# A CIN tower on one core: three fp32r passes for four of six first-layer chunks, an earlier warm-up and VectorE chain, and rows put in place by SyncE's transfers

## The chip, the cores and the metric

The kernel runs on one core of a Trainium2 chip, as one launch. The core has TensorE (matmuls into PSUM), VectorE, ScalarE, GpSimd, SyncE (here only as an issuer of transfers) and 16 DMA engines; SBUF and PSUM have 128 partitions each. The metric is the device time of the launch in microseconds, the median of several runs. A profiled execution has its own time, given beside its span.

## The reference, cut to what is computed

```python
e = jnp.stack([tbl_f[ids[:, f]] for f in range(39)], axis=1)      # (1024, 39, 16)
x1 = relu(einsum('bhd,bmd,shm->bsd', e, e, W1) + b1)              # S = 128
x2 = relu(einsum('bhd,bmd,shm->bsd', x1, e, W2) + b2)             # S = 128
z  = concatenate([x1.sum(-1), x2.sum(-1)], axis=-1)               # (1024, 256)
h = concatenate([z, dense_ctx], axis=1)                           # + 16 columns
h = maximum(h @ W_top1 + b_top1, 0)                               # 512
h = maximum(h @ W_top2 + b_top2, 0)                               # 256
y = h @ W_top3                                                    # (1024, 1)
```

All of it is fp32.

## The kernel before

**Tiles.** The batch is cut into 32 tiles of 32 examples. A tile has 32 x 16 = 512 columns of (example, embedding position) for the first layer. For the second layer it is two "pairs" (p = 2t even, 2t + 1 odd) of two blocks ("sub") of 128 columns each. A pair is the unit of every engine's main loop.

**Rows.** GpSimd looks up the embedding rows with indirect DMAs into `looked` (ten for a tile, 64 bytes a row; L339). A row then has to be put in place, into `e`, where positions are spread over partitions: 16 copies of 32 partitions x 40 elements for a tile (`put_in_place`, L290). For tiles 0 and 1 VectorE does eight of them (L561) and ScalarE eight (L464); for later tiles ScalarE does all 16. Tiles are put, split into high and low parts and multiplied in "fills": one tile a fill up to tile 7, two tiles up to 19, four tiles from 20 (`FILLS`). A fill is worked at the even pair two tiles ahead of its first tile: ScalarE puts at slots 1, 3, 4 and makes the high part after slot 5; VectorE computes products after its D bank 4 (L570) and the low parts after D bank 5 (L580, L583).

**First layer.** The 741 products of two fields left after 15 that are made directly are written as squares of sums: TensorE expands x0t with a selection matrix into one of six chunks (`expand`, L690, fp32r, 512 columns), ScalarE squares it from PSUM to SBUF (`square`, L444), and TensorE multiplies it with the weights in fp32 (`layer1`, L702) into the bank BK_ACC1. Expand(t, v+1) and layer1(t, v) follow each other on TensorE, two slots after expand(t, v). All expansions, the turn of the next tile (`turn`, L678), the sums and the dense layers share one PSUM bank, BK_T: `staging` makes each use wait until the one before it has been read. After the last chunk ScalarE makes x1h and x1 (L450, L453), VectorE x1l (L595, after D bank 3 of the even pair).

**Second layer.** For each of 39 fields TensorE multiplies x1 with W2 in three fp32r passes (x1h w2h, x1h w2l, x1l w2h; L724 to L726), four fields to a bank. Of the ten banks of a pair seven (27 fields, "D") are scaled and added up by VectorE (L634, one multiply-add of 128 columns for each field and sub, `acc`), and three (12 fields, "A") are scaled by ScalarE into `fy` (L425) and added by GpSimd (L348) into `fsum`, with which VectorE's chain starts. The order on TensorE is the string `ORDER = "DDADDADDAD"`, ten slots a pair; the A banks are made one pair and one bank ahead. Banks go through a ring of three: bank n waits until bank n - 3 has been read. First-layer steps stand in every second slot: expansions of chunks 0 to 4 in slots 1, 3, 5, 7, 9 of the odd pair, chunk 5 in slot 1 of the next even pair, and the last layer1 in slot 3.

**Start.** TensorE folds the weights (L761), turns tile 0, runs its first layer, and then makes the banks A0, A1, A2 of pair 0 and the first A bank of pair 1 before the loop. VectorE splits W2 into w2h and w2l in between (L588, L590).

**Dense layers.** They run for examples 0 to 511 in tiles 17 and 18, for 512 to 895 in tiles 29 and 30, the rest at the end (`MLP_AT`).

## Time and profile before

| | us |
|---|---|
| median of 3 runs (1232.1 to 1232.55) | 1232.25 |
| the profiled execution | 1228.31 |
| its span | 1226.4 |
| TensorE busy | 1172.4 (96%) |
| VectorE busy | 1005.4 (82%) |
| ScalarE busy | 672.1 (55%) |
| GpSimd busy | 864.8 (71%) |

The busy shares are averages over the span. The chain of work that ended last says which engine's work stood where the end was set. The order of time lists instructions of an engine with start and length, merged where they follow each other without a pause; an idle time before one is given in brackets with what ended it. A length holds the pipeline's tail, so the distance of two starts is the cost of one where they are packed. A matmul's column count stands behind its partitions.

### The profile page before, as it was taken

What the parts mean: (1) busy time and instruction counts of PE and PEld (TensorE: products, weight loads), DVE (VectorE), ACT (ScalarE), POOL (GpSimd) and SP (SyncE); (2) the same over time, 40 slices, a digit from 0 to 9 for tenths busy, and PEclk for the clock granted to TensorE, in tenths of its full rate; (3) what the DMA queues carried; (4) which work ended last, traced back from release to release, by engine and by line L of the source; (5) the groups of instructions that cost most, each with busy time, mean ns of one, the idle gap of its engine ahead of it and who ended that gap; (6) DMA issues with size and microseconds to landing.
All of it is one profiled execution on the core that took longest, in us unless ns stands there. A gap on an engine that the chain in (4) does not pass through costs nothing.

```text
span 1226.4 us, 17749 instructions
## 1 busy us (share of the span) xinstructions
PE 1172.4 (96%) x4784; PEld 879.4 (72%) x4784; DVE 1005.4 (82%) x3692; ACT 672.1 (55%) x2188; POOL 864.8 (71%) x836
## 2 busy tenths in 40 slices
PE   3899999999999999999999999999999999999996
PEld 2577777777777777777776667777777777777775
DVE  4298898888899888888896678888888888887695
ACT  2656666665565656556564465555655565545430
POOL 7888878888888788788776757888886454444350
PEclk9899999999999999999999999999999999999997
DMA  5000000000000000000000000000000000000000
GB/s 177 5 4 4 4 4 3 4 4 5 3 4 3 4 3 3 4 4 3 4 4 3 3 3 3 4 3 4 3 4 2 1 1 1 1 1 1 1 1 1
DMA packets 12801, 9.08 MB, mean 7 GB/s; under 512 B 6190, under 2 KB 11822, under 8 KB 12573
## 3 DMA queue, kind: packets, MB, share of 16 engines
q0 software_dynamic: 10240, 2.64, 2.6%
q1 hardware_dynamic: 2461, 5.31, 1.3%
q8 instruction: 38, 0.62, 0.2%
q14 instruction: 62, 0.51, 0.1%
HBM read 7.92 MB, written 0.00 MB: 6 GB/s over the span
## 4 chain that ended last, share of the span: by engine, by line
PE 72%; DVE 18%; ACT 5%; issue 2%; POOL 2%; DMA 0%; SPq 0%; ACTq 0%
PE ps L724 17%; PE ps L726 17%; PE ps L725 17%; DVE acc L634 15%; PE ps L702 13%; PE ps L690 3%; PE ps L755 3%; ACT e L464 2%; ACT fy L425 2%; POOL looked L339 2%; DVE x1l L595 1%; PE ps L678 1%; DVE e_hl L580 1%; PE ps L697 0%; DVE e_hl L583 0%
## 5 line engine op out<-in xcount | busy, mean ns | idle before, releaser
L634 DVE SCALAR_TENSOR_TENSOR acc<-ps,e,acc 128x128 f32<-128x128 f32 x3200 | 854.4, 343 | 155.7 <-PE ps L726 152.4
L724 PE MATMUL ps<-w2h,x1h 128*128 128x512 f32 (+1 forms) x1280 | 582.4, 455 | 24.9 <-ACT fy L425 13.8
L348 POOL TENSOR_TENSOR fy<-fy 128x512 f32<-128x512 f32 (+1 forms) x256 | 403.0, 1574 | 214.3 <-ACT fy L425 193.5
L425 ACT ACTIVATE fy<-ps,e 128x128 f32<-128x128 f32 x1536 | 418.1, 387 | 198.8 <-PE ps L726 198.3
L726 PE MATMUL ps<-w2h,x1l 128*128 128x512 f32 (+1 forms) x1280 | 495.4, 387 | 0.0
L725 PE MATMUL ps<-w2l,x1h 128*128 128x512 f32 (+1 forms) x1280 | 494.3, 386 | 0.0
L339 POOL DMA_INDIRECT looked<-in_table,rows x320 | 310.9, 972 | 79.1 <-issue 55.0
L724 PEld LDWEIGHTS ps<-w2h,x1h 128*128 128x128 f32 x1280 | 241.5, 189 | 134.1 <-DVE acc L634 50.9
L725 PEld LDWEIGHTS ps<-w2l,x1h 128*128 128x128 f32 x1280 | 241.6, 189 | 82.6 <-issue 44.7
L726 PEld LDWEIGHTS ps<-w2h,x1l 128*128 128x128 f32 x1280 | 240.7, 188 | 48.4
L444 ACT ACTIVATE z<-ps 128x512 f32<-128x512 f32 x192 | 117.9, 614 | 224.8 <-PE ps L690 219.5
L702 PE MATMUL ps<-z,w_sb 128*128 128x512 f32 x384 | 198.8, 599 | 0.0
L702 PEld LDWEIGHTS ps<-z,w_sb 128*128 128x128 f32 x384 | 73.4, 192 | 16.6 <-ACT z L444 1.7
L690 PE MATMUL ps<-x0t,sel_r 78*128 78x512 f32 x186 | 74.0, 398 | 2.7 <-ACT z L444 1.8
L464 ACT ACTIVATE e<-looked 32x40 f32<-32x40 f32 (+5 forms) x256 | 67.3, 263 | 13.7 <-DMA looked<-in_table,rows 7.8
L348 POOL TENSOR_TENSOR fy<-fy,b_sb 128x256 f32<-128x256 f32 x64 | 47.7, 746 | 18.8 <-ACT fy L425 17.8
L634 DVE SCALAR_TENSOR_TENSOR acc<-ps,e,fsum 128x128 f32<-128x128 f32 x128 | 38.8, 344 | 26.0 <-POOL fsum L348 16.8
L348 POOL TENSOR_TENSOR fsum<-fy 128x256 f32<-128x256 f32 x64 | 47.5, 743 | 10.8 <-POOL fy L348 4.4
L690 PEld LDWEIGHTS ps<-x0t,sel_r 78*128 78x128 f32 x186 | 34.9, 188 | 10.9 <-ACT z L444 3.5
L634 DVE SCALAR_TENSOR_TENSOR ps<-ps,e,acc 128x128 f32<-128x128 f32 x128 | 38.9, 350 | 0.0
L432 ACT ACTIVATE x0t<-ps 128x512 fp32r<-128x512 f32 x32 | 19.4, 605 | 30.5 <-PE ps L678 30.5
L678 PE MATMUL ps<-ident_sb,e_hl 128*128 128x128 f32 x128 | 20.9, 287 | 9.1 <-DVE e_hl L583 8.8
(64 smaller groups left out, 385.5 us busy)
## 6 DMA issues: line engine op xcount, KB each, us to landing
looked<-in_table,rows POOLq DMA_INDIRECT x320, 2.3
w_st<-in_w SPq DMA_DIRECT2D x1, 1728.0 KB, 10.2
wt_sb<-in_wt SPq DMA_DIRECT2D x2, 512.0 KB
w_st<-in_w SPq DMA_DIRECT2D x1, 768.0 KB, 6.3
w_sb<-in_w1a SPq DMA_DIRECT2D x1, 448.0 KB, 3.2
w1b_sb<-in_w1b SPq DMA_DIRECT2D x1, 448.0 KB, 3.8
...
```

What stands on the lines that cost most here:

```text
L339: nc.gpsimd.indirect_dma_start(looked[:, t % LOOKED, j, :], None, table, bass.IndirectOffsetOnAxis(rows[:, t, j:j + 1], 0)).then_inc(s_loo ...
L348: nc.gpsimd.tensor_tensor(out, a, b, ALU.add).then_inc(s_fsum, 1)
L425: nc.scalar.activation(fy[:, p % 2, sub, m - MD, :], ps[:, 2 * (nth % RING) + sub, k * S:(k + 1) * S], ACT.Copy, scale=emb(p, sub, m)).the ...
L444: nc.scalar.activation(z1[:, k % 2, :], src, ACT.Square).then_inc(s_z1, 1)
L464: nc.scalar.activation(*put_in_place(f, k, q), ACT.Copy).then_inc(s_put_act, 1)
L634: nc.vector.scalar_tensor_tensor(acc[:, sub, :] if m < MD - 1 else y, y, emb(p, sub, m), acc[:, sub, :] if m else fsum[:, p % 2, sub, :], ...
L690: nc.tensor.matmul(ps[:, BK_T, :], sel_r[:, v, :], x0t[0:2 * M, t % 2, :], start=True, stop=True).then_inc(s_full, 1)
L702: nc.tensor.matmul(ps[:, BK_ACC1, :], w1_sb[:, v, :], z1[:, k % 2, :], start=False, stop=(v == C1 - 1)).then_inc(s_mm1, 1)
L724: nc.tensor.matmul(y, x1h[:, t % 2, at], w2h[:, cols], start=True, stop=False)
L725: nc.tensor.matmul(y, x1h[:, t % 2, at], w2l[:, cols], start=False, stop=False)
L726: mm = nc.tensor.matmul(y, x1l[:, t % 2, at], w2h[:, cols], start=False, stop=True)
L755: mm = nc.tensor.matmul(y, w, x, start=(k == 0), stop=(k == len(terms) - 1))
```

## The change

- **Three passes.** For tiles from 2 on, chunks 0, 2, 3, 5 of the first layer (`SPLIT`) are no longer multiplied in fp32. The weights are split once into w1h and w1l (fp32r), the squares into zh (ScalarE, fp32r) and zl: ScalarE squares a second time in place in PSUM (`s_sq`), and VectorE subtracts zh from it into zl (`square_low`). TensorE then does w1h zh + w1l zh + w1h zl. `staging` waits for VectorE's subtraction (`s_zl`) in these chunks. `split_after` puts the subtraction into VectorE's program after a D bank: D bank 1, 3 and 5 of the odd pair for chunks 0, 2, 3, and D bank 1 of the even pair for chunk 5.
- **Warm-up and first banks.** 28 matmuls of 512 columns with no use stand before turn(0). The order of banks of pair 0 is new: A0, D0, A1, D1, A2 before the loop, then nine more. For the first two pairs (`LATE`) VectorE's chain starts with a multiplication and adds fsum later, before its last field. The first bank waits for x1l only at its third matmul. The split of W2's A part is shared: ScalarE makes w2h, VectorE w2l.
- **Rows.** For tiles from 2 on SyncE puts the rows in place with 16 DMAs a tile from `looked` to `e`, after the tile's look-ups; ScalarE, VectorE and GpSimd wait for `s_put`.
- **Moved.** Dense-layer steps stand in other slots; hid1, hid2 and y_sb lie in the memory of w2_st.

```diff
+SPLIT, SPLIT_FROM = (0, 2, 3, 5), 2
+LATE = 2
+WARM = 28
...
-    slots = [[("A", 0, a) for a in range(A_BANKS)] + [("A", 1, a) for a in range(EARLY)]]
-    for p in range(PAIRS):
+    slots = [[("A", 0, 0), ("D", 0, 0), ("A", 0, 1), ("D", 0, 1), ("A", 0, 2)]]
...
+    for p in range(1, PAIRS):
...
+def split_after(p, j):
+
+    slots = [s for s, kind in enumerate(ORDER) if kind == "D"] + [SLOTS]
+    return [at for s in range(slots[j], slots[j + 1]) for at in layer1_steps(p, s) if is_split(*at)]
...
-    for c, s in enumerate((0, 4, 14, 16)):
+    for c, s in enumerate((0, 4, 8, 14)):
...
-    MLP_AT[TILE_SLOTS * (tile + 1) + 14] = (g, 3, 0)
+    MLP_AT[TILE_SLOTS * (tile + 1) + 8] = (g, 3, 0)
...
+                for t in range(FIRST_TILES, TILES):
+                    sp.wait_ge(s_look[t], 16 * LOOKUPS)
+                    for k in range(Q):
+                        for q in range(Q):
+                            sp.dma_start(*put_in_place(t, k, q)).then_inc(s_put[t - FIRST_TILES], 16)
...
-                    nc.scalar.activation(z1[:, k % 2, :], src, ACT.Square).then_inc(s_z1, 1)
+                    if is_split(t, v):
+                        nc.scalar.activation(zh[:, k % 2, :], src, ACT.Square).then_inc(s_z1, 1)
+                        nc.scalar.activation(src, src, ACT.Square).then_inc(s_sq, 1)
+                    else:
+                        nc.scalar.activation(z1[:, k % 2, :], src, ACT.Square).then_inc(s_z1, 1)
...
+                def square_low(t, v):
+                    k = C1 * t + v
+                    dve.wait_ge(s_sq, splits(t, v))
+                    if k >= 2:
+                        dve.wait_ge(s_mm1, k - 1)
+                    nc.vector.tensor_tensor(zl[:, k % 2, :], ps[:, BK_T, :], zh[:, k % 2, :], ALU.subtract).then_inc(s_zl, 1)
...
+                            if m == MD - 1 and p < LATE:
+                                dve.wait_ge(s_fsum, ADDS_PER_PAIR * (p + 1))
+                                dve.wait_ge(s_stt, n)
...
+                        for at in split_after(p, j):
+                            square_low(*at)
...
-                            pe.wait_ge(s_z1, C1 * at[0] + at[1] + 1)
+                            if is_split(*at):
+                                pe.wait_ge(s_zl, splits(*at))
+                            else:
+                                pe.wait_ge(s_z1, C1 * at[0] + at[1] + 1)
...
+                    if is_split(t, v):
+                        nc.tensor.matmul(ps[:, BK_ACC1, :], w1h[:, v, :], zh[:, k % 2, :], start=False, stop=False)
+                        nc.tensor.matmul(ps[:, BK_ACC1, :], w1l[:, v, :], zh[:, k % 2, :], start=False, stop=False)
+                        pe.wait_ge(s_zl, splits(t, v))
+                        mm = nc.tensor.matmul(ps[:, BK_ACC1, :], w1h[:, v, :], zl[:, k % 2, :], start=False, stop=(v == C1 - 1))
...
+                for _ in range(WARM):
+                    nc.tensor.matmul(ps[:, C1 - 1, :], sel_r[:, 0, :], sel_r[:, 0:N // K1, :].rearrange("p c k -> p (c k)"),
+                                     start=True, stop=True)
```

TensorE, odd pair 1, from the last matmuls of bank D2 over the expansion of chunk 1 of tile 2 and the multiplication of chunk 0 to bank D3 (ps is PSUM, z the squares, sel_r the selection matrix; the semaphores an instruction waits for stand in brackets). Before:

```order
L724 MATMUL ps<-w2h,x1h 128x512
L725 MATMUL ps<-w2l,x1h 128x512
L726 MATMUL ps<-w2h,x1l 128x512
L690 MATMUL ps<-x0t,sel_r 128x512 [waits s_z1]
L702 MATMUL ps<-z,w_sb 128x512 [waits s_z1]
L724 MATMUL ps<-w2h,x1h 128x512 [waits s_stt]
```

Now:

```order
L796 MATMUL ps<-w2h,x1h 128x512
L797 MATMUL ps<-w2l,x1h 128x512
L800 MATMUL ps<-w2h,x1l 128x512
L752 MATMUL ps<-x0t,sel_r 128x512 [waits s_zl]
L765 MATMUL ps<-zh,w1h 128x512 [waits s_z1]
L766 MATMUL ps<-zh,w1l 128x512
L768 MATMUL ps<-zl,w1h 128x512 [waits s_zl]
L796 MATMUL ps<-w2h,x1h 128x512 [waits s_stt]
```

The expansion waits for s_zl, VectorE's subtraction, where it waited for s_z1, ScalarE's square, and three matmuls stand for one.

VectorE, the same pair, banks D0, D1 and D2. Before:

```order
L634 SCALAR_TENSOR_TENSOR acc<-ps,e,fsum 128x128 [waits s_stt,s_fsum,s_y]
L634 SCALAR_TENSOR_TENSOR acc<-ps,e,fsum 128x128 [waits s_stt,s_fsum]
L634 SCALAR_TENSOR_TENSOR acc<-ps,e,acc 128x128 [waits s_stt] x6
L634 SCALAR_TENSOR_TENSOR acc<-ps,e,acc 128x128 [waits s_stt,s_y]
L634 SCALAR_TENSOR_TENSOR acc<-ps,e,acc 128x128 [waits s_stt] x7
L634 SCALAR_TENSOR_TENSOR acc<-ps,e,acc 128x128 [waits s_stt,s_y]
```

Now (L688 multiplies, L691 multiplies and adds, L633 is the subtraction):

```order
L688 TENSOR_SCALAR acc<-ps,e 128x128 [waits s_stt,s_y]
L688 TENSOR_SCALAR acc<-ps,e 128x128 [waits s_stt]
L691 SCALAR_TENSOR_TENSOR acc<-ps,e,acc 128x128 [waits s_stt] x6
L691 SCALAR_TENSOR_TENSOR acc<-ps,e,acc 128x128 [waits s_stt,s_y]
L691 SCALAR_TENSOR_TENSOR acc<-ps,e,acc 128x128 [waits s_stt] x7
L633 TENSOR_TENSOR zl<-ps,zh 128x512 [waits s_mm1,s_sq]
L691 SCALAR_TENSOR_TENSOR acc<-ps,e,acc 128x128 [waits s_stt,s_y]
L691 SCALAR_TENSOR_TENSOR acc<-ps,e,acc 128x128 [waits s_stt] x7
```

The subtraction stands between bank D1 and bank D2 and waits for ScalarE's second square.

VectorE, the first banks of pair 0. Before:

```order
L583 TENSOR_TENSOR e_hl<-prod,e_hl 128x60 [waits s_eh]
L634 SCALAR_TENSOR_TENSOR acc<-ps,e,fsum 128x128 [waits s_fsum,s_y]
L634 SCALAR_TENSOR_TENSOR acc<-ps,e,fsum 128x128 [waits s_fsum]
L634 SCALAR_TENSOR_TENSOR acc<-ps,e,acc 128x128 [waits s_stt] x6
L634 SCALAR_TENSOR_TENSOR acc<-ps,e,acc 128x128 [waits s_stt,s_y]
```

Now:

```order
L620 TENSOR_TENSOR e_hl<-prod,e_hl 128x60 [waits s_eh]
L688 TENSOR_SCALAR acc<-ps,e 128x128 [waits s_y]
L688 TENSOR_SCALAR acc<-ps,e 128x128
L691 SCALAR_TENSOR_TENSOR acc<-ps,e,acc 128x128 [waits s_stt] x6
L691 SCALAR_TENSOR_TENSOR acc<-ps,e,acc 128x128 [waits s_stt,s_y]
L691 SCALAR_TENSOR_TENSOR acc<-ps,e,acc 128x128 [waits s_stt] x7
```

The wait for s_fsum is gone from the chain's head; only the bank itself (s_y) is waited for.

## Rows read from the trace of the kernel before

**Rows 1.** The page's busy line, and the chain's shares by engine.
```profile
PE 1172.4 (96%) x4784; PEld 879.4 (72%) x4784; DVE 1005.4 (82%) x3692; ACT 672.1 (55%) x2188; POOL 864.8 (71%) x836
...
PE 72%; DVE 18%; ACT 5%; issue 2%; POOL 2%; DMA 0%; SPq 0%; ACTq 0%
```

**Rows 2.** The chain in time: start us, us, what; VectorE's multiply-adds, every second pair.
```profile
380.22 1.96 DVE acc L634 x8
...
415.09 1.96 DVE acc L634 x8
...
451.06 1.96 DVE acc L634 x8
```

**Rows 3.** Order of time, TensorE, an ordinary tile: start us, us, engine, line, operation.
```profile
458.08 0.50 PE L724 MATMUL ps<-w2h,x1h 128*128 128x512 f32 x1 [0.27 <-DVE acc L634]
...
461.44 0.40 PE L690 MATMUL ps<-x0t,sel_r 78*128 78x512 f32 x1
...
464.64 0.40 PE L690 MATMUL ps<-x0t,sel_r 78*128 78x512 f32 x1
...
464.87 1.02 PE L702 MATMUL ps<-z,w_sb 128*128 128x512 f32 x2
...
465.96 0.40 PE L725 MATMUL ps<-w2l,x1h 128*128 128x512 f32 x1
...
475.82 0.40 PE L690 MATMUL ps<-x0t,sel_r 78*128 78x512 f32 x1
```

**Rows 4.** Order of time, VectorE, the same tile.
```profile
453.14 0.68 DVE L595 SCALAR_TENSOR_TENSOR x1l<-ps,x1h 128x512 fp32r<-128x512 f32 x1
...
453.80 5.26 DVE L634 SCALAR_TENSOR_TENSOR acc<-ps,e,acc 128x128 f32<-128x128 f32 x20
...
460.01 0.60 DVE L634 SCALAR_TENSOR_TENSOR acc<-ps,e,fsum 128x128 f32<-128x128 f32 x2
...
471.13 4.23 DVE L634 SCALAR_TENSOR_TENSOR acc<-ps,e,acc 128x128 f32<-128x128 f32 x16 [1.66 <-PE ps L726]
```

**Rows 5.** Order of time, a fill of two tiles: VectorE, then TensorE's expand(t, 1).
```profile
422.17 1.17 DVE L580 TENSOR_TENSOR e_hl<-e,e_hl 128x312 f32<-128x312 f32 x1
...
423.25 0.82 DVE L583 TENSOR_TENSOR e_hl<-prod,e_hl 128x120 f32<-128x120 f32 x1
...
426.07 0.60 DVE L634 SCALAR_TENSOR_TENSOR acc<-ps,e,fsum 128x128 f32<-128x128 f32 x2
...
429.76 0.40 PE L690 MATMUL ps<-x0t,sel_r 78*128 78x512 f32 x1
```

**Rows 6.** Order of time, a fill of one tile: VectorE, then TensorE's expand(t, 1).
```profile
107.58 0.60 DVE L634 SCALAR_TENSOR_TENSOR acc<-ps,e,fsum 128x128 f32<-128x128 f32 x2
...
111.52 0.40 PE L690 MATMUL ps<-x0t,sel_r 78*128 78x512 f32 x1
```

**Rows 7.** Order of time, a fill of four: VectorE, then TensorE's expand(t, 1).
```profile
871.22 0.60 DVE L634 SCALAR_TENSOR_TENSOR acc<-ps,e,fsum 128x128 f32<-128x128 f32 x2
...
875.38 0.40 PE L690 MATMUL ps<-x0t,sel_r 78*128 78x512 f32 x1
```

**Rows 8.** The start: a stretch with its granted clock (0.50), then order of time.
```profile
37.00:38.30 1.30, 1.30 (x4) 0.99 (x3) 0.99 (x5) 1.18 (x6) 0.99 (x2) 0.50 0.10 8
...
38.99 6.30 ACT L425 ACTIVATE fy<-ps,e 128x128 f32<-128x128 f32 x24
...
56.06 0.61 DVE L634 SCALAR_TENSOR_TENSOR acc<-ps,e,fsum 128x128 f32<-128x128 f32 x2 [16.76 <-POOL fsum L348]
...
73.01 0.40 PE L690 MATMUL ps<-x0t,sel_r 78*128 78x512 f32 x1
```

**Rows 9.** Transfers: the look-ups' queue, two issues of SyncE, the last look-up of tile 2.
```profile
q0 software_dynamic: 10240, 2.64, 2.6%
...
18.81 0.90 SPq L327 DMA_DIRECT2D wt_sb<-in_wt  x2
...
46.54 0.94 POOL L339 DMA_INDIRECT looked<-in_table,rows  x1 [0.30 <-issue]
```

151 lines of the change are left out of this document (91 added, 60 removed).

## The prediction

> **What bounds the kernel now.** I read the page's busy shares first, then the chain of work that ended last, then the order of time on TensorE and VectorE over two tiles. [rows 1] TensorE is busy 96% of the span and holds 72% of the chain; VectorE is busy 82% and holds 18%. That reads like a TensorE-bound kernel, and for such a kernel cheaper matmuls are worth their full saving. But 18% of the chain is VectorE, so a part of each tile is set by it. [rows 2] gives the tile's period: the same point of every second pair comes at 380.22, 415.09 and 451.06, so 34.87 us for a tile without a fill ahead of it and 35.97 us for one with a fill of two tiles.
>
> I call T the start of expand(t, 0), which follows the second D bank of an odd pair. [rows 3] In an ordinary tile T is 461.44. TensorE then wants expand(t, 1) at 464.64, T + 3.20, and expand(t, 4) at 475.82. [rows 4] VectorE starts D bank 0 of that pair at 460.01, T - 1.43. One multiply-add costs 5.17/20 = 0.2585 us (20 of them from 453.80 to 458.97, the row's 5.26 less its overlapping end), so a D bank of eight is 2.07 us against 1.37 us for TensorE to make one. VectorE ends D bank 1 at 460.01 + 4.14 = 464.15. This lag, not the busy share, is what the change meets.
>
> **Three passes for one fp32 matmul.** [rows 3] One fp32r matmul of 512 columns is 0.23 us (464.64 to 464.87). From 464.87 to 465.96 stand the fp32 matmul and one fp32r matmul, so the fp32 one is 1.09 - 0.23 = 0.86. Three passes are 0.68: 0.18 saved, 4 x 30 tiles = 120 times, 21.6 us if nothing else moves.
>
> What it adds: 120 squares on ScalarE, written back to the PSUM bank (of the size of those already there, on a ScalarE that is 55% busy and loses its copies; only the subtraction waits for them), and 120 subtractions on VectorE of 128x512 from PSUM. That operation is not in the trace; x1l has its shape and its kinds of operands, and takes 453.80 - 453.14 = 0.66 us [rows 4]. I take 0.66. The bounds: x1l and a multiply-add of 128 columns differ by 384 columns and 0.40 us, so 512 columns without any fixed part are 0.53; four multiply-adds of 128 columns would be 1.03. In sum 79 us more for VectorE.
>
> **The added wait.** There is one staging bank (BK_T). Before, expand(v+1) waits until ScalarE has squared chunk v; that is done while the next bank is multiplied. Now it waits for VectorE's subtraction, which stands in VectorE's program behind a D bank. Queued behind that expand on TensorE are all further banks. A release from VectorE costs TensorE about 0.25 us: D bank 5 ended at 453.80 + 16 x 0.2585 = 457.94 and the bank that waited for it started at 458.08, with its first matmul some 0.11 longer [rows 3, 4]. The four places, in an ordinary tile:
> - chunk 0: VectorE ends D bank 1 at 464.15, subtraction 464.81, release 465.06, wanted 464.64. Lost 0.42.
> - chunk 2: VectorE starts D bank 4 at 471.13 after an idle gap of 1.66 us [rows 4]; the subtraction fits there. Lost 0.
> - chunk 3: it stands behind D bank 5. From 471.13 (now 0.24 later) two banks and a subtraction end at 476.17, release 476.42. TensorE, with 0.42 - 0.18 - 0.18 behind it, wants it at 475.88. Lost about 0.55.
> - chunk 5: it stands behind D bank 1 of the even pair; three banks later TensorE only just finds it ready. Lost 0, and the 0.18 saved counts, because VectorE waits for the bank behind it. (The wait for D bank 5 at the next pair's first bank, the idle 0.27 in [rows 3], stays.)
> Sum: 0.97 lost against 0.72 saved, so +0.25 us in an ordinary tile.
>
> **After a fill it is worse**, since VectorE enters the odd pair later and before the ring of three banks hid most of it. For each kind I take VectorE's start of D bank 0, add 4.14 + 0.66 + 0.25, and compare with the time at which TensorE took expand(t, 1) before:
> - fill of two [rows 5]: the low parts run from 422.17 to 424.00; 426.07 + 5.05 = 431.12 against 429.76: 1.36 lost. Over the ordinary 0.42 that is 0.94 more, so +1.19 a tile, 6 tiles: +7.1.
> - fill of one [rows 6]: 107.58 + 5.05 = 112.63 against 111.52: 1.11 lost, +0.94 a tile, 5 tiles: +4.7.
> - fill of four [rows 7]: 871.22 + 5.05 = 876.27 against 875.38: 0.89 lost, +0.72, 2 tiles: +1.4. The copies that ScalarE made there go, but behind them VectorE's chain is next in line, so they give nothing here.
> - ordinary: 12 tiles x 0.25 = +3.0.
> - the four tiles with dense-layer steps: TensorE has extra work, VectorE time to spare; the moved steps give slack at one place and take it at another. Taken as 0, between -2 and +2.
> Together +16.2 us.
>
> The low parts have a price of their own in this: [rows 5] 128x312 takes 1.08 us (422.17 to 423.25) where its size would ask for about a third. If that time vanished in the new kernel's timing, a fill would cost 0.7 less, 11 x 0.7 = 8 us.
> The Trainium skill's page "SBUF — State Buffer", section "SBUF: two separate sides", gives a reason: an operation of VectorE with two SBUF inputs and a GpSimd operation take one port pair in turn, each for its whole length. By that rule the length stays as it is, since GpSimd's additions keep their place; without it the sum would be 8 us lower. No run here shows which.
>
> **The start.** [rows 8] VectorE's first multiply-add stands at 56.06, after 16.76 us of idle time for GpSimd's fsum; T of the first odd pair is 73.01. Now D banks come between the A banks and need no fsum. What is late next: put(1) hangs on the look-ups, and ScalarE reads its first bank at 38.99 whatever TensorE did before. So the 28 warm-up matmuls and the earlier first bank are worth little: TensorE makes banks A0, D0, A1 by about 36, then waits until ScalarE's bank has been read, at 38.99 + 6.30/3 = 41.1, and the granted clock may be down by then (0.50 from 37.0 to 38.3 [rows 8]). The warm-up stands in a stretch in which TensorE waits for turn(0) anyway; if all 28 ran at half clock, 0.46 us each, and ended some us after turn(0) could start, the same wait for ScalarE would hide it. From 41.1 on TensorE has D1, turn(1), A2, the seven chunks of tile 1, nine more banks and D0, D1 of pair 1: 1.3 for the slow clock, 0.5 + 6.8 + 0.5 for turns and chunks, 13 banks at 1.37 less 0.3, and about 1.3 of waits for ScalarE's squares while it scales A2: 28 us, T at about 69. Gain 4 us; bounds 0 (the clock stays down through these gaps) and 8 (none of the waits).
>
> **Rows put in place by SyncE.** Per tile 16 DMAs of 320 runs of 16 bytes; ScalarE loses its copies of tiles 2 to 31, which stood on no end-setting path except in fills of four. [rows 9] Two issues of SyncE take 0.90, so 16 take 7.2 us, plus about 2.3 to land. Tile 2's look-ups end at about 49.8: in place at 59.3, wanted by VectorE (products after D bank 4) near 61. Later tiles have a pair, some 17 us, to spare. So 0 is the price taken. It is bounded from above by the runs: 10,240 packets of four rows took 2.6% of 16 engines, 510/10,240 = 0.05 us a packet, 0.0125 a row. At 0.0125 a run a tile's 5,120 runs take 4 us on 16 engines; at a whole packet's 0.05 they take 16 us, and tile 2 is 7 us late. SyncE's queue holds nothing else but the output.
> The Trainium skill speaks against this part: "DMA: Bandwidth & Descriptors", section "Specifications", says that below 512 bytes a transfer is a read-modify-write. By that rule 16-byte runs lie at the dear end, and the sum would be 7 us higher; its section "Why small descriptors are slow (HBM only)" says that transfers within SBUF are spared, which would leave 0. No transfer within SBUF is in this trace.
>
> **The sum.** 1228.31 (profiled execution, span 1226.4) - 4 + 16.2 = 1240.5. The median of the runs is 1232.25, 3.9 above the profiled one; 1232.25 + 12.2 = 1244.
>
> **The rivals.**
> A. TensorE alone sets the pace: the subtractions find gaps everywhere (VectorE idles 155 us in all), 21.6 + 4 are gained: 1207. For it: 96% busy. Against it: VectorE's gaps lie behind D bank 1 and ahead of D bank 4, while three of four subtractions are wanted elsewhere [rows 4].
> B. The waits are only half paid, because VectorE's low parts shorten or because releases come at 0.14 and not 0.25: 16.2 - 8 - 6, near +2, with the start -2: 1230, from 1225 to 1236.
> C. Slower still: the puts land late. It decides from a put of more than 9 us a tile; at 16 us tile 2 is 7 us late and VectorE stands at products(2), at 32 us, close to the 34.9 us period, it is 23 us late and the next fills follow. 1244 + 7 to 20, taken as 1255.
> My own forecast ends above the time before, A below.
>
> **Chances.** Forecast 0.60 (its own range, with start and low parts at their bounds, 1234 to 1254), A 0.16, B 0.12, C 0.12. A measurement of this kernel tells 0.2%, 2.5 us, from no change. Faster: all of A, half of B, a little of mine: 0.23. Same: 0.07. Slower: 0.70. The range that leaves out two in ten cuts most of A and the end of C: 1216 to 1258.
>
> **What would show it.** Right: VectorE busy near 1085 us; TensorE's busy time a little down yet its idle time up, the expansion (now line 752) waiting for VectorE's subtraction about twice a tile for 0.4 to 1.4 us; tile periods of about 35.1, and near 37.1 where a fill of two precedes; VectorE's first multiply near 41; the copies' landing ahead of line 607. Wrong: expansions that never wait and a period of 34.2 (A); high_part or products waiting for a DMA (C); first T later than 73. The step I trust least is the carry of a fill's lateness into the odd pair, the most secure the 0.66 us of the subtraction.

## The result, and the profile after

The changed kernel takes 1262.18 us (median of four, 1260.91 to 1264.23) against 1232.4 (four, 1232.1 to 1233.03): ratio 1.0243, 95% interval 1.0225 to 1.026. It is slower, as forecast, but by 30 us where 12 were forecast, and the time lies above the range of 1216 to 1258. The profiled execution is the one of 1260.91, its span is 1259.1.

The page of the changed kernel: busy time by engine, the SyncE queue's packets, the shares of the chain, and groups of instructions (busy, mean ns | idle before, and what ended it). The answers of before are in [rows 1].

```profile
PE 1175.3 (93%) x4932; PEld 905.1 (72%) x4932; DVE 1090.3 (87%) x3816; ACT 667.0 (53%) x2070; POOL 866.0 (69%) x836
...
q1 hardware_dynamic: 159901, 7.73, 7.1%
...
PE 52%; DVE 38%; issue 6%; ACT 2%; POOL 1%; another core or an unknown queue 0%; DMA 0%; SPq 0%; DVEq 0%; ACTq 0%
...
L796 PE MATMUL ps<-w2h,x1h 128*128 128x512 f32 (+1 forms) x1280 | 535.0, 418 | 39.5 <-DVE acc L691 29.4
...
L633 DVE TENSOR_TENSOR zl<-ps,zh 128x512 fp32r<-128x512 f32 x120 | 81.8, 682 | 21.3 <-ACT ps L480 20.8
L752 PE MATMUL ps<-x0t,sel_r 78*128 78x512 f32 x186 | 79.8, 429 | 19.6 <-DVE zl L633 10.0
```

The subtraction costs 682 ns (forecast 0.66 us), and VectorE is busy 1090 (forecast 1085). TensorE's busy time rose from 1172.4 to 1175.3; without the 6.8 of the warm-up matmuls it fell by 3.9. Its share of the chain went from 72% to 52%, VectorE's from 18% to 38%. Part of TensorE's new idle time stands where the forecast put it, at the expansion (L752). There it waits 35 times for the subtraction, 1.0 us at the most. More stands at L796, the first pass of a bank, and it is VectorE's banks that release it: 29.4 us. In before that was 7.9.

Where the time went is read from T, the start of the matmul that follows expand(t, 0), once a tile. Two pairs of rows of that line on TensorE (start, duration), of the changed kernel: behind a fill of one, and in an ordinary tile.

```profile
156.21 0.39 PE L759 MATMUL ps<-x0t,wz 128*128 128x512 f32 x1
...
193.81 0.39 PE L759 MATMUL ps<-x0t,wz 128*128 128x512 f32 x1
...
832.53 0.39 PE L759 MATMUL ps<-x0t,wz 128*128 128x512 f32 x1
...
867.56 0.39 PE L759 MATMUL ps<-x0t,wz 128*128 128x512 f32 x1
```

That is 37.60 us behind a fill of one, against 35.15, and 35.03 in an ordinary tile, against 34.84 (836.17 - 801.33). The forecast had 36.1 and 35.1. The first T of an odd pair is 82.45 against 73.25, where 69 was forecast (its counterpart of 73.01; the two lines stand 0.24 apart). Of the 32.6 us between the two profiled executions 9.2 lie ahead of the first T of an odd pair, 12.6 in the six periods behind it (five fills of one, the first of two) and 11.3 in the next ten (five fills of two); the others together add nothing. So the ordinary tile came out right, the fills and the start did not. Here is one fill of the changed kernel, all engines that matter (start, duration, engine, line):

```profile
148.15 0.95 POOL L371 DMA_INDIRECT looked<-in_table,rows  x1 [0.30 <-issue]
...
148.89 1.62 DVE L607 TENSOR_TENSOR prod<-e 128x60 f32<-128x60 f32 x1
...
149.10 2.72 POOL L380 TENSOR_TENSOR fy<-fy 128x512 f32<-128x512 f32 x2
...
150.43 2.15 DVE L691 SCALAR_TENSOR_TENSOR acc<-ps,e,acc 128x128 f32<-128x128 f32 x8
...
152.50 0.40 DVE L617 TENSOR_TENSOR e_hl<-e,e_hl 128x156 f32<-128x156 f32 x1
...
152.63 0.50 PE L796 MATMUL ps<-w2h,x1h 128*128 128x512 f32 x1 [1.80 <-DVE acc L691]
```

The product of 60 elements takes 1.62 us; in before it takes 0.21. It stands ahead of D bank 5, and that bank holds the PSUM that TensorE's next bank needs: TensorE idles 1.80 us.

### The profile page after: what moved, and what is told of

Read it like the earlier page. It is cut to its first block, busy times and chain, and to the rows that moved or that the text cites. A ratio compares the mean times of both kernels' runs of the same rounds, so it can differ in the third digit from the quotient of the medians.

```text
span 1259.1 us, 18613 instructions
## 1 busy us (share of the span) xinstructions
PE 1175.3 (93%) x4932; PEld 905.1 (72%) x4932; DVE 1090.3 (87%) x3816; ACT 667.0 (53%) x2070; POOL 866.0 (69%) x836
## 4 chain that ended last, share of the span: by engine, by line
PE 52%; DVE 38%; issue 6%; ACT 2%; POOL 1%; another core or an unknown queue 0%; DMA 0%; SPq 0%; DVEq 0%; ACTq 0%
DVE acc L691 31%; PE ps L796 12%; PE ps L800 11%; PE ps L797 11%; PE ps L770 4%; PE ps L752 4%; PE ps L829 3%; DVE zl L633 3%; PE ps L765 2%; PE ps L768 2%; PE ps L766 2%; DVE prod L607 2%; DVE x1l L637 1%; ACT fy L459 1%; POOL looked L371 1%
## 5 line engine op out<-in xcount | busy, mean ns | idle before, releaser
L691 DVE SCALAR_TENSOR_TENSOR acc<-ps,e,acc 128x128 f32<-128x128 f32 x3200 | 852.5, 342 | 82.7 <-PE ps L800 71.7
L796 PE MATMUL ps<-w2h,x1h 128*128 128x512 f32 (+1 forms) x1280 | 535.0, 418 | 39.5 <-DVE acc L691 29.4
L796 PEld LDWEIGHTS ps<-w2h,x1h 128*128 128x128 f32 x1280 | 242.0, 189 | 123.8 <-DVE acc L691 57.8
L479 ACT ACTIVATE zh<-ps 128x512 fp32r<-128x512 f32 x120 | 71.7, 598 | 211.8 <-PE ps L752 187.1
L633 DVE TENSOR_TENSOR zl<-ps,zh 128x512 fp32r<-128x512 f32 x120 | 81.8, 682 | 21.3 <-ACT ps L480 20.8
L752 PE MATMUL ps<-x0t,sel_r 78*128 78x512 f32 x186 | 79.8, 429 | 19.6 <-DVE zl L633 10.0
L770 PE MATMUL ps<-z,w_sb 128*128 128x512 f32 x144 | 75.9, 609 | 0.0
L480 ACT ACTIVATE ps<-ps 128x512 f32<-128x512 f32 x120 | 71.1, 593 | 0.0
L752 PEld LDWEIGHTS ps<-x0t,sel_r 78*128 78x128 f32 x186 | 34.8, 187 | 47.3 <-DVE zl L633 28.3
L482 ACT ACTIVATE z<-ps 128x512 f32<-128x512 f32 x72 | 45.5, 632 | 20.5 <-PE ps L752 12.9
L691 DVE SCALAR_TENSOR_TENSOR acc<-ps,e,fsum 128x128 f32<-128x128 f32 x124 | 37.6, 344 | 17.3 <-PE ps L800 7.7
L765 PE MATMUL ps<-zh,w1h 128*128 128x512 f32 x120 | 47.8, 398 | 0.0
```

The costliest lines, as they stand in the source:

```text
L479: nc.scalar.activation(zh[:, k % 2, :], src, ACT.Square).then_inc(s_z1, 1)
L633: nc.vector.tensor_tensor(zl[:, k % 2, :], ps[:, BK_T, :], zh[:, k % 2, :], ALU.subtract).then_inc(s_zl, 1)
L691: nc.vector.scalar_tensor_tensor(acc[:, sub, :] if m < MD - 1 else y, y, emb(p, sub, m), acc[:, sub, :] if m else fsum[:, p % 2, sub, :], ...
L752: nc.tensor.matmul(ps[:, BK_T, :], sel_r[:, v, :], x0t[0:2 * M, t % 2, :], start=True, stop=True).then_inc(s_full, 1)
L765: nc.tensor.matmul(ps[:, BK_ACC1, :], w1h[:, v, :], zh[:, k % 2, :], start=False, stop=False)
L770: mm = nc.tensor.matmul(ps[:, BK_ACC1, :], w1_sb[:, v, :], z1[:, k % 2, :], start=False, stop=(v == C1 - 1))
```

## What each kernel showed

All kernels of this study by the same places. The ratio is to the kernel before, run on the same chip between them. Its median was 1232.4 beside the changed kernel, 1232.1 beside undo_passes, only_passes, only_puts and only_start, 1232.7 beside copies_twice and the three mid_ kernels, and 1227.0 or 1227.2 beside all others. First T is that of the first odd pair; "one" is the period from the fifth T to the sixth, behind a fill of one; "two" the two tiles with one fill of two (tenth T to twelfth); "ordinary" from the 23rd to the 24th; "four" the next, behind a fill of four. All in us of the profiled execution.

| kernel | ratio (95%) | first T | one | two | ordinary | four |
|---|---|---|---|---|---|---|
| before | 1 | 73.25 | 35.15 | 70.85 | 34.84 | 36.25 |
| after | 1.0243 (1.0225-1.026) | 82.45 | 37.60 | 72.70 | 35.03 | 36.73 |
| undo_passes | 1.0105 (1.0075-1.0134) | 84.99 | 36.35 | 71.42 | 34.86 | 36.40 |
| only_passes | 1.0181 (1.0149-1.0212) | 79.20 | 36.19 | 72.27 | 35.00 | 38.48 |
| only_puts | 1.0055 (1.0035-1.0075) | 76.67 | 36.32 | 71.42 | 34.87 | 37.97 |
| only_start | 1.0058 (1.0035-1.0081) | 88.15 | 35.14 | 70.80 | 34.86 | 36.21 |
| only_mlp | 0.9988 (0.9976-0.9999) | 72.42 | 35.15 | 70.83 | 34.87 | 36.21 |
| puts_prod_early | 1.0148 (1.0095-1.02) | 72.89 | 38.23 | 71.82 | 34.87 | 36.95 |
| passes_mid | 0.9912 (0.9883-0.9941) | 73.12 | 34.82 | 70.12 | 34.25 | 36.16 |
| no_warm | 1.0226 (1.0197-1.0256) | 75.45 | 37.71 | 72.80 | 35.01 | 36.73 |
| after_mid | 1.0066 (1.0043-1.0089) | 75.39 | 37.32 | 71.62 | 34.25 | 37.50 |
| puts_two_waits | 1.0054 (1.0031-1.0077) | 73.49 | 36.32 | 71.40 | 34.87 | 36.41 |
| only_warm | 1.0006 (0.9995-1.0017) | 71.77 | 35.12 | 70.82 | 34.86 | 36.20 |
| only_order | 1.0026 (1.0012-1.004) | 79.22 | 35.12 | 70.82 | 34.86 | 36.20 |
| copies_twice | 0.9979 (0.9967-0.9991) | 78.27 | 35.14 | 70.83 | 34.89 | 36.25 |
| mid_0 | 1.0015 (1.0004-1.0026) | 77.18 | 35.22 | 71.03 | 34.67 | 36.59 |
| mid_03 | 0.9895 (0.9867-0.9924) | 77.58 | 34.86 | 70.12 | 34.25 | 36.19 |
| mid_2late | 0.9953 (0.9934-0.9973) | 76.98 | 35.06 | 70.53 | 34.46 | 36.42 |
| puts_add_waits | 0.9972 (0.996-0.9984) | 72.26 | 35.15 | 70.80 | 34.86 | 36.06 |
| all_mended | 0.9859 (0.9842-0.9875) | 72.58 | 34.83 | 69.90 | 34.22 | 35.43 |

A caution for "first T": where the kernel before ran at 1232, kernels with its start have it some 5 us later (copies_twice 78.27) than where it ran at 1227 (only_mlp 72.42). The profiled execution of before, 3.9 under its median, is of the latter kind. First T is compared only within a kind: the changed kernel's 82.45 belongs beside the 78.27 of copies_twice, not beside 73.25.

A caution for "four" too. After much the same wait TensorE's granted clock fell in some of these periods and not in others, whatever the kernel. In only_passes TensorE waits 2.21 us for ScalarE in both fills of four. After the first wait the clock was 0.50, the lower level of 1.2 GHz, for some 3 us; after the second it stayed at 1.00 (a stretch; busy time and instructions of TensorE, its weight loads, VectorE, ScalarE and GpSimd; granted clock; DMA share and GB/s):

```profile
888.47 0.55 PE L801 MATMUL ps<-w2h,x1h 128*128 128x512 f32 x1 [2.21 <-ACT fy L462]
...
1032.69 0.47 PE L801 MATMUL ps<-w2h,x1h 128*128 128x512 f32 x1 [2.21 <-ACT fy L462]
```

```profile
889.00:892.00 3.00, 3.00 (x10) 2.52 (x9) 2.77 (x3) 1.36 (x6) 2.69 (x3) 0.50 0.00 0
1033.00:1036.00 3.00, 3.00 (x16) 2.65 (x15) 3.00 (x5) 2.42 (x11) 2.69 (x3) 1.00 0.00 0
```

Ten matmuls stand where 16 do at the full clock. This is in the 38.48 of only_passes (its second fill of four took 36.93, where before took 36.22) and in the 37.97 of only_puts (clock 0.52 from 881 to 884.5; puts_two_waits took 36.41); both are some 1.5 too long as a price of the kernel. The 37.50 of after_mid holds such a stretch too (0.50 from 883 to 886). No other value of the column does.

## One part at a time

Theory M: the start and VectorE's subtractions are the loss. Rivals: SyncE's transfers, or the extra preparation.

**undo_passes:** the changed kernel, no chunk split, w1h and w1l not made.

```diff
-SPLIT, SPLIT_FROM = (0, 2, 3, 5), 2
+SPLIT, SPLIT_FROM = (), 2
```

> All parts of the change but the three passes (no chunk is split, and w1h and w1l are not made). Theory M (the loss of about 30 us is 9 at the start and the rest from VectorE's subtractions behind the banks and the fills): the start's 9 us stays, the period of every tile goes back to that of before, 34.9 ordinary and 35.15 after a fill of one: 1241, within 3. Rival S (SyncE's transfers of 16-byte runs disturb the other engines' access to SBUF, and the fills' lateness comes from them): periods after fills of one stay near 37, 1250 or more. Rival D (the start's delay comes from the extra preparation of w1h and w1l, 7 us of instructions on ScalarE and VectorE): near 1233.

**only_passes:** the changed kernel with the bank order, the prologues and the copies by ScalarE and VectorE as before; left of the change are the passes and the dense-layer steps.

```diff
-LATE = 2
+LATE = 0
-PUT_DVE, PUT_ACT = (0, 1), (2, 3)
+def put_by_act(f):
+    return tuple(k for k in range(Q) if k not in put_by_dve(f))
```

> Only the three passes, with the dense-layer steps where the change has them; the start and the copies are those of before. Theory M: the steady loss alone, 1232 + 23 = 1255, first T of an odd pair at 73 to 75 as before. Rival S: without SyncE's transfers the product of a fill is short again and the periods after fills are about 1 us shorter than in the changed kernel: 1245. The forecast of the record for this part was 16 us, 1248.

**only_puts:** as only_passes, but no chunk split and SyncE's transfers.

```diff
+                for t in range(FIRST_TILES, TILES):
+                    sp.wait_ge(s_look[t], 16 * LOOKUPS)
```

> Only SyncE's transfers in place of ScalarE's copies of tiles 2 to 31. Theory M: no effect, 1232 within 2; where a fill of four stands, ScalarE has room and the time may fall by 1. Rival S: slower by 5 to 12.

**only_start:** the changed kernel with no chunk split and copies by ScalarE.

```diff
+LATE = 2
+WARM = 28
```

> Only the start: 28 warm-up matmuls, pair 0's banks in the new order, b2's sum added late, ScalarE making the first part of w2h. Theory M: 1232 + 9 = 1241, x0t of tile 0 at about 25.7 after a wait of 5 us. Rival D: x0t at 22.2 as before and 1228 to 1232, the delay then belongs to what the passes add to the preparation.

Measured: 1244.56, 1253.95, 1238.07 and 1239.56 against 1232.11. Each part costs something: passes 22, transfers 6, start 7.5, the dense-layer steps in all of them -1.5 (below). The forecast took the transfers at 0 and the start at -4. Rival S has half a point: the transfers do cost, and they cost at the fills, 1.2 us each behind a fill of one (36.32 against 35.15), nothing in ordinary tiles. Rival D falls: without w1h and w1l the start is as late (84.99, 88.15). The parts, with the dense-layer steps counted once, sum to 38 against 30 for the whole. By the profiled executions some 4 of the difference are the start, which costs less once ScalarE has no copies (first T 79.22 in only_order, 75.39 in after_mid), some 2 the tiles with dense-layer steps (2.9 longer in only_passes than in only_mlp, 0.9 in the changed kernel than in undo_passes), and some 3 the lower clock in two of the kernels. Why the dense-layer tiles differ was not tried.

**only_mlp:** the kernel before with the dense-layer steps moved.

```diff
-    for c, s in enumerate((0, 4, 14, 16)):
+    for c, s in enumerate((0, 4, 8, 14)):
-    MLP_AT[TILE_SLOTS * (tile + 1) + 14] = (g, 3, 0)
+    MLP_AT[TILE_SLOTS * (tile + 1) + 8] = (g, 3, 0)
```

> The kernel before with nothing but the dense-layer steps moved (slots 14 and 16 to 8 and 14, and 14 to 8 in the next tile). In the traces of the kernels with a part of the change, the first period with such steps is 2.2 longer and the two behind it are 2.5 each shorter, and the tail is 3.3 shorter. Theory: the move alone gains 4 to 6: 1227. The forecast on record took 0 with bounds of 2: 1230 to 1234. A second profile of the start of the kernel before: the profiled execution so far (1228.31) was 2 to 4 under the others, so I expect its first T of an odd pair 2 to 4 later than 73.25, with ScalarE's stretch near 43 to 49 slow as in the kernels with a part of the change.

Measured: 1225.17 against 1227.17. It gains 2, less than the 4 to 6 read from the traces, and the forecast's bounds of 2 held.

## The place of the subtractions

**passes_mid:** only_passes, with MID = (0, 3, 5).

```diff
                                 n += 1
+                            if k == 1:
+                                for at in split_after(p, j):
+                                    if at[1] in MID:
+                                        square_low(*at)
                         for at in split_after(p, j):
-                            square_low(*at)
+                            if at[1] not in MID:
+                                square_low(*at)
```

> The three passes alone, as in only_passes, with VectorE's subtractions for chunks 0, 3 and 5 placed two fields into their D bank instead of behind it, 1.0 us sooner. Theory M (TensorE loses 0.4 to 1.4 us per tile at the expansions because the staging bank is released too late): the waits of the expansions vanish, an ordinary period goes from 35.0 to 34.3, one behind a fill of one from 36.2 to about 35: 1254 falls by 20 to 25, 1229 to 1234. Rival V (VectorE's 79 us of added work are the loss, wherever they stand): no change, 1250 or more.

Measured: 1216.85 against 1227.17, faster than the kernel before. VectorE does the same work (busy 1078.5); only three subtractions a tile stand 1.0 us sooner. Rival V falls. TensorE's waits, first of only_passes and then of passes_mid (in total, times, longest):

```profile
PE ps L760 <- DVE zl L639: 20.8, 46, 1.3
PE ps L801 <- ACT fy L462: 20.5, 15, 5.2
```

```profile
PE ps L807 <- ACT fy L463: 17.8, 17, 2.2
...
PE ps L807 <- DVE acc L700: 8.4, 24, 1.2
```

Of the expansions' 46 waits for zl one is left, of 0.2 us. T of passes_mid in an ordinary tile:

```profile
932.16 0.40 PE L773 MATMUL ps<-x0t,wz 128*128 128x512 f32 x1
...
966.41 0.39 PE L773 MATMUL ps<-x0t,wz 128*128 128x512 f32 x1
```

34.25 is 0.6 under before, of the 0.72 that four times 0.18 promise. The gain in all, 33 us by the ratios, is more than I expected, but near what the forecast's own terms say if all its waits go: 16.2 of loss become 21.6 of gain, 37.8.

**mid_0** has MID = (0,), **mid_03** MID = (0, 3). **mid_2late** has MID = (0, 3, 5) and chunk 2's subtraction in D bank 4:

```diff
+                            if k == 0 and j == 4:
+                                for at in split_after(p, 3):
+                                    square_low(*at)
```

> The three passes alone, with only chunk 0's subtraction two fields into its D bank. By the steps of the record chunk 0 loses 0.42 in an ordinary tile and up to 1.36 after a fill, chunk 3 0.55. Theory T (the waits are in series and one takes over from the other: TensorE freed at chunk 0 comes to chunk 3 sooner and waits there for what it gained): of the 33 us less than 12 come off, all of it behind fills: ratio to the kernel before 1.008 or more. Rival I (each place has its own loss): 24 off, near 0.998.

> As mid_0 with chunk 3 moved too; chunk 5 stays behind its bank. Theory T: nearly all of the 33 us are off, 0.991 to 0.993, since chunk 5 was worked out as losing nothing. If chunk 5 takes over as well: 0.997 or more.

> As passes_mid, with the one subtraction that waits for ScalarE (chunk 2's, 19 us of VectorE in sum, 33 times) moved one field into D bank 4 so that it finds the square ready. Theory: VectorE had idle time there anyway in ordinary tiles, so nothing in those; behind fills VectorE is short of time and gains up to 0.5 each, 13 fills: 0 to 6 us under passes_mid, 0.987 to 0.992. Rival: the expansion of chunk 3 now waits for it: slower.

Measured: 1234.17, 1219.19 and 1226.16 against 1232.7. From 1.0181 chunk 0 takes off 20 us, chunk 3 another 15, chunk 5 nothing that can be told (0.9895 and 0.9912, intervals overlap). Chunk 0 alone was worked out as 0.42 x 30 tiles and the fills' 12, 24.7; chunk 3 as 0.55 x 30 = 16.5. Rival I is the nearer: the losses are in series but each place keeps most of its own. In mid_0 the ordinary period is 34.67, and TensorE still waits for zl 31 times:

```profile
PE ps L766 <- DVE zl L640: 6.3, 31, 0.5
```

mid_2late goes the rival's way. VectorE's wait for ScalarE at the subtraction falls from 19.0 to 0.9 us, but the weight loads of the expansions now wait 14.0 us for zl instead of 5.6, and the ordinary period is 34.46 instead of 34.25. By the ratios it is 5 us slower than passes_mid; their intervals just touch.

**after_mid:** the changed kernel with passes_mid's edit.

```diff
+MID = (0, 3, 5)
+                            if k == 1:
+                                for at in split_after(p, j):
+                                    if at[1] in MID:
+                                        square_low(*at)
```

> The whole changed kernel, with VectorE's subtractions for chunks 0, 3 and 5 two fields into their D bank, as in passes_mid. There the same edit took 37 us off, against 24 expected. Theory M (the place of the subtractions is the main loss of the change, whatever its other parts): from 1.024 of the kernel before to about 0.998, 25 to 35 us less. Rival F (with SyncE's transfers VectorE's product waits for GpSimd at every fill, and VectorE then has no slack that an earlier subtraction could use): less than 15 us off, 1.012 or more.

Measured: 1235.19 against 1227.02, ratio 1.0066: 22 us come off the whole change, between the two theories. Ordinary tiles gain all (34.25), but the period behind a fill of one only 0.3 (37.32). There something else rules.

## The fills: who holds the port

**puts_prod_early:** only_puts, the product inside D bank 4.

```diff
+                            if k == 2 and j == 4 and fill is not None:
+                                products(fill)
-                        if fill is not None and j == 4:
-                            products(fill)
```

> SyncE's transfers alone, as in only_puts, with VectorE's product of a fill placed three fields into D bank 4 instead of behind it, 0.5 us sooner, while GpSimd still issues a look-up and not yet adds. Theory P (the transfers themselves cost nothing; the 1.2 a fill comes from the product, which starts within 0.03 us of GpSimd's addition and now loses: 1.45 us instead of 0.21): the product takes 0.21 to 0.28 again, the period after a fill of one goes from 36.33 back to 35.15, and the time falls by 5 to 10 against only_puts: 1228 to 1233. Rival S (16-byte runs slow VectorE's SBUF accesses): the product stays over 1 us and the period at 36.3, 1238.

**puts_two_waits:** only_puts, in products(f).

```diff
+                    if tiles.start >= FIRST_TILES:
+                        dve.wait_ge(s_put_act, Q * len(PUT_ACT) * FIRST_TILES)
```

> As only_puts, with one more wait on the product of each fill, on a semaphore that has long had its value. In the kernels with ScalarE's copies the product waits on two semaphores, for the copies of both engines, and takes 0.21; with SyncE's transfers it waits on one and takes 1.45, with the same distance to GpSimd's look-up and addition (0.91 and 0.90 behind the look-up's start). Theory N (the form of the wait decides which engine gets the SBUF port first): the product is back at 0.21 to 0.28 and the period after a fill of one at 35.15, 5 to 8 us less than only_puts. Rival G (something else that comes with SyncE's transfers): 36.3 and no change.

**copies_twice:** only_mlp's kernel (the kernel before with the moved steps), and on SyncE 16 transfers a tile (its queue and the look-ups wait for them):

```diff
+                    for k in range(Q):
+                        for q in range(Q):
+                            sp.dma_start(e_copy[q * BT:(q + 1) * BT, k:M:Q, :],
...
```

> The kernel before (with the moved dense-layer steps), ScalarE's copies kept, and SyncE's 16 transfers for every tile 2 to 31 on top, into a tile that nothing reads. Theory Q (the presence of SyncE's transfers makes VectorE's product wait for GpSimd): the product takes 1.45 and the period after a fill of one is 36.3; 7 us slower than the kernel before. Theory R (ScalarE without its copies runs ahead, or the product of rows that a transfer wrote is what waits): the product stays at 0.21, the period at 35.15, within 2 us of the kernel before.

Measured: 1244.93 against 1227.17, 1234.0 against 1227.02, 1229.9 against 1232.7. Theories P, N and Q fell. Placed sooner the product became slower, 1.94 us. A second wait changed nothing (1.44). With SyncE's transfers and ScalarE's copies together it stayed at 0.21, so the presence of the transfers is not the cause. Two readings are left in R: ScalarE runs ahead without its copies, or a product of rows that a transfer wrote is slow. What tells the cases apart is on GpSimd and ScalarE. Around one product, in the timeline of before, of only_puts and of puts_prod_early:

```profile
100.22 2.18 ACT L425 ACTIVATE fy<-ps,e 128x128 f32<-128x128 f32 x8
...
101.56 0.94 POOL L339 DMA_INDIRECT looked<-in_table,rows  x1 [0.30 <-issue]
...
102.47 0.21 DVE L570 TENSOR_TENSOR prod<-e 128x60 f32<-128x60 f32 x1
102.52 1.32 POOL L348 TENSOR_TENSOR fy<-fy 128x512 f32<-128x512 f32 x1
```

```profile
139.04 2.18 ACT L457 ACTIVATE fy<-ps,e 128x128 f32<-128x128 f32 x8 [1.67 <-PE ps L787]
...
141.58 0.95 POOL L369 DMA_INDIRECT looked<-in_table,rows  x1 [0.30 <-issue]
142.48 1.45 DVE L599 TENSOR_TENSOR prod<-e 128x60 f32<-128x60 f32 x1
142.55 2.71 POOL L378 TENSOR_TENSOR fy<-fy 128x512 f32<-128x512 f32 x2
```

```profile
98.90 2.18 ACT L458 ACTIVATE fy<-ps,e 128x128 f32<-128x128 f32 x8 [1.68 <-PE ps L788]
...
101.42 0.94 POOL L370 DMA_INDIRECT looked<-in_table,rows  x1 [0.30 <-issue]
101.82 1.94 DVE L600 TENSOR_TENSOR prod<-e 128x60 f32<-128x60 f32 x1
102.38 2.70 POOL L379 TENSOR_TENSOR fy<-fy 128x512 f32<-128x512 f32 x2
```

In before ScalarE ends its scaled fields at 102.40, and GpSimd's addition, which waits for them, starts at 102.52: it is released just as the look-up ends. The product that began at 102.47 is done in 0.21. In the other two ScalarE, rid of its copies, ended at 141.22 and 101.08: the addition stood released behind the look-up. There the product loses, although its record starts 0.07 and even 0.56 us ahead of the addition's, and it ends within 0.1 us of the first of the two additions. Theory L, formed from this: an addition that is released already and stands behind a look-up keeps VectorE's two-input operation out before it starts itself.

Two rows bound this. The look-up alone does not keep the product out: in the changed kernel's first fill the product begins in a look-up that another look-up follows, and takes 0.21:

```profile
65.92 0.96 POOL L371 DMA_INDIRECT looked<-in_table,rows  x1
67.18 0.94 POOL L371 DMA_INDIRECT looked<-in_table,rows  x1 [0.30 <-issue]
...
66.61 0.21 DVE L607 TENSOR_TENSOR prod<-e 128x60 f32<-128x60 f32 x1
```

And an addition released long before does not claim the port at any distance. In puts_prod_early's first fill ScalarE had ended at 65.72, the product began 0.28 us into the look-up and 0.68 ahead of the addition, and it was not kept out, while those that began 0.40 into it were:

```profile
66.18 0.94 POOL L370 DMA_INDIRECT looked<-in_table,rows  x1 [0.31 <-issue]
67.14 1.30 POOL L379 TENSOR_TENSOR fy<-fy 128x512 f32<-128x512 f32 x1
...
66.46 0.21 DVE L600 TENSOR_TENSOR prod<-e 128x60 f32<-128x60 f32 x1
```

**puts_add_waits:** only_puts, in GpSimd's last_fields(p).

```diff
+                    if p % 2 and p // 2 + 2 in FILL_AT:
+                        pool.wait_ge(s_prod, FILL_AT[p // 2 + 2] + 1)
```

> As only_puts, with one wait more on GpSimd: its addition behind the second look-up of an odd pair's fields waits until VectorE's product of the fill is done. Theory L (an addition that is released already and stands behind a look-up keeps VectorE's product out from before its own start): the product takes 0.21 to 0.28 again although it starts in the same look-up, the addition starts 0.1 to 0.3 later, the period behind a fill of one goes from 36.33 to 35.2, and the ratio to the kernel before from 1.0055 to about 0.999. Rival K (the product is slow for a reason of its own): product 1.45, and now the addition behind it late as well: 1.006 or more.

Measured: 1223.46 against 1226.95. One fill in its timeline:

```profile
135.52 0.94 POOL L369 DMA_INDIRECT looked<-in_table,rows  x1 [0.30 <-issue]
136.42 0.21 DVE L601 TENSOR_TENSOR prod<-e 128x60 f32<-128x60 f32 x1
...
136.72 1.29 POOL L378 TENSOR_TENSOR fy<-fy 128x512 f32<-128x512 f32 x1 [0.25 <-DVE prod L601]
```

Same look-up, same distance of 0.90, and the product takes 0.21; the period is 35.15 again. So it is GpSimd's addition that the product waits for, and not the rows that a transfer wrote; a wait more on GpSimd makes the kernel 10 us faster than only_puts. That the addition's early release is what lets it win, as theory L has it, is read from the rows above; when it takes the port no record shows. The Trainium skill, page "SBUF — State Buffer", section "SBUF: two separate sides", says that VectorE with two SBUF inputs and GpSimd share one port pair as an exclusive lock and that whichever starts first gets it for its whole instruction. The length of the waits agrees: a product that loses ends within 0.1 us of an addition's end. By the records the one that starts first does not always get it.

## The start

**no_warm:** the changed kernel without the warm-up.

```diff
-WARM = 28
+WARM = 0
```

> The changed kernel without the 28 warm-up matmuls. Theory W (at 0.44 us each they run 12.3 us, until about 24.6, and hold up turn(0), which could start at 20.7): x0t of tile 0 at 22.2 instead of 25.7 and the time 3 to 4 shorter, 1258.5. Rival A (the stretch to 49 is set by something at a fixed time, the end of the look-ups): x0t earlier but the first T of an odd pair within 1 us of 82.45, time unchanged at 1262. Rival C (the warm-up did raise the clock for the first layer): the first layer of tile 0 takes longer, 1262 or more.

**only_warm:** the kernel before, with the warm-up ahead of turn(0).

```diff
+                for _ in range(28):
+                    nc.tensor.matmul(ps[:, C1 - 1, :], sel_r[:, 0, :],
...
```

> The kernel before plus 28 warm-up matmuls ahead of turn(0), nothing else. Theory W: they end at about 24.6 and x0t of tile 0 comes 3.5 us later, the first layer is no faster: 3 to 4 us slower in total. Rival C (they raise TensorE's clock for the first layer and the first banks): the first layer, 9.9 us from the first expansion to x1h, gets 2 us shorter, and the total is 0 to 2 us slower.

**only_order:** only_start without the warm-up.

```diff
-WARM = 28
+WARM = 0
```

> The start without the warm-up: the banks of pair 0 in the new order, GpSimd's sum added late, w2h's first part by ScalarE, and the moved dense-layer steps; copies and fp32 as before. Forecast of the record: first T of an odd pair 4 us sooner than 73. Theory O (interleaved in one ring of three, each bank waits for the other engine's and for fills that come between; only_start's first T of an odd pair was 88.15, of which the warm-up holds 3.7): 80 or more, and the time 3 to 8 us slower than the kernel before with the moved dense-layer steps.

Measured: 1254.6 against 1227.17, 1227.56 and 1231.05 against 1227.02. The warm-up is worth nothing either way in only_warm (1.0006), and no_warm's 1.0226 can't be told from the change's 1.0243. Theory W does not hold there; it came from only_start and undo_passes, whose warm-up took this long, first only_start, then only_warm:

```profile
12.65 12.32 PE L848 MATMUL ps<-sel_r 78*128 78x512 f32 x28
```

```profile
12.32 7.08 PE L766 MATMUL ps<-sel_r 78*128 78x512 f32 x28
```

0.44 us each, until 24.97, or 0.25 each, until 19.4. In the first case turn(0), which could start near 20.7, stands behind it. So the warm-up's price is 0 or some 3.5 us by the execution. In the changed kernel's trace the records end at 19.04, yet ScalarE reads turn(0)'s result only at 25.74, as in only_start (25.85); which of the two it was can't be told.

The rest of the new start is the dear part (the order of pair 0's banks, GpSimd's sum added late, and ScalarE's share of w2h; these three were not tried apart): only_order less only_mlp is 0.38%, 4.7 us, and its first T is 79.22 against 72.42. With SyncE's transfers it is less, 75.39 in after_mid. In after_mid VectorE begins at 40.18, as forecast, but its chain then meets the fill of tile 2. Its rows, and TensorE's wait in the same kernel:

```profile
63.73 2.38 DVE L618 TENSOR_TENSOR e_hl<-e,e_hl 128x156 f32<-128x156 f32 x1 [1.05 <-ACT e_hl L506]
66.20 1.23 DVE L621 TENSOR_TENSOR e_hl<-prod,e_hl 128x60 f32<-128x60 f32 x1
```

```profile
PE ps L802 <- DVE p L716: 5.1, 1, 5.1
```

The low parts wait for ScalarE's high part and then stretch over GpSimd's additions (3.79 us from 63.56), 4.7 us with the wait. Pair 0's last bank stands behind them, and TensorE idles 5.1 us at the edge of the pairs. Its granted clock is 0.50 from 71 to 73 behind this idle time. In only_order it idles 4.35 us there and runs at 0.50 from 73 to 78.5, which costs half of that stretch:

```profile
73.00:78.50 5.50, 5.50 (x15) 4.43 (x16) 2.16 (x8) 0.60 (x1) 4.66 (x9) 0.50 0.01 2
```

This is part of why only_order's first T is later than after_mid's. VectorE's sooner start bought idle time: in its timeline it waits for TensorE's banks four times before this, 0.61 to 5.17 us each.

## All parts, mended

**all_mended:** the changed kernel (SyncE's transfers, SPLIT, the dense-layer steps) with the start of the kernel before, passes_mid's edit and GpSimd's wait of puts_add_waits.

```diff
-LATE = 2
+LATE = 0
+MID = (0, 3, 5)
...
+                    if p % 2 and p // 2 + 2 in FILL_AT:
+                        pool.wait_ge(s_prod, FILL_AT[p // 2 + 2] + 1)
```

> The change with each part that lost mended: the start of the kernel before (no warm-up, pair 0's banks and sums in the old order), three subtractions two fields into their banks, GpSimd's addition behind the product, SyncE's transfers and the moved dense-layer steps kept. Theory: the passes gain as in passes_mid (ordinary period 34.24, 34.8 behind a fill of one), the transfers cost nothing, a fill of four gains up to 1 because ScalarE's copies are gone: ratio 0.987 to 0.992. Rival F (VectorE, 94% busy in such tiles, is held by GpSimd's later additions at the low parts instead): periods behind fills over 35.5, ratio over 0.995.

Measured: 1210.01 against 1226.95, ratio 0.9859 (0.9842 to 0.9875), better than expected and 17 us faster than the kernel before. Its page and its longest wait of TensorE:

```profile
PE 1156.0 (96%) x4904; PEld 896.0 (74%) x4904; DVE 1075.1 (89%) x3813; ACT 666.2 (55%) x2069; POOL 864.3 (72%) x836
...
PE 72%; DVE 22%; POOL 3%; issue 2%; ACT 1%; DMA 0%; SPq 0%; POOLq 0%; DVEq 0%
```

```profile
PE ps L797 <- DVE acc L690: 15.2, 39, 1.2
```

The chain is TensorE's again, 72%. Behind a fill of four 35.43 stands against 36.16 of passes_mid, of which the next tile gives back 0.4 (35.01 against 34.60). By the ratios it is 6.5 us faster than passes_mid. Whether the transfers or GpSimd's wait bring that was not separated: passes_mid with the wait alone was not run.

## The prediction, point by point

- **What bounds it.** Right: the lag of VectorE and not the busy shares decided; rival A, TensorE alone, did not come. (Its 155 us are the idle time ahead of one group; VectorE idles 221 in all.)
- **Ordinary tile, +0.25.** Right within 0.1: 0.16 to 0.19. That the loss sits at chunks 0 and 3 and not at 5 held; by mid_0 and mid_03 they are worth 20 and 15 us where the terms gave 24.7 and 16.5.
- **Fills, as far as the passes go.** Right: only_passes is 1.04 longer behind a fill of one (0.94), and 1.42 over the two tiles of a fill of two (1.19 + 0.25). Behind a fill of four 0.71 (0.72) where the clock stayed up, 2.2 where it fell.
- **"If that time vanished".** Here the step on the port failed. I held the low parts' length fixed and did not ask what ScalarE, without its copies, would do to GpSimd's additions. They are released sooner, the wait for the port moves from the low part (0.78 us in before, 0.40 in the changed kernel) to the product (0.21, now 1.62), and the product stands ahead of a bank that TensorE needs: 1.2 a fill of one, 0.6 a fill of two.
- **SyncE's transfers at 0.** Wrong for that reason, and not for the bounds that I had worked out. The transfers land in time: neither ScalarE nor VectorE waits for one. The issue of 16 takes 10.45 us and more (forecast 7.2), and 1.9 us to land. The cost was in the removal of the copies, which I had priced as removing nothing.
- **The start, -4.** Wrong in sign: the new order with its late sum costs 4.7 us, the warm-up 0 or 3.5. The failed step is the sum that ran to T = 69 over TensorE's work and left out the fill of tile 2, which stands in VectorE's chain ahead of pair 0's last bank. "What is late next" had no answer for VectorE. The lower clock behind the idle time that this makes was not in the sum either.
- **Dense-layer steps at 0 (2 either way).** Right, -2.
- **The sum.** The mis-sized terms are the transfers (0, measured 6, or 7.5 without the dense-layer gain that only_puts holds) and the start (-4, measured 7.5, or 9); the passes' 16.2 came out as 22 to 24. In the profiled executions, against only_mlp, the excess is 2.9 in the tiles with dense-layer steps, taken at 0 for the passes, 1.7 behind the last T and in the last period, and 2.8 at the fills of four, with the lower clock in it. The transfers and the start are the larger part of the miss. That the whole came out slower, as forecast, rests on the passes, which alone cost 22. Rival C came nearest in time, 1255, by a mechanism that did not occur.
